# Joining the attention sums with the normalised rows: one addition moves from TensorE to GpSimd

## The chip, the cores and the metric

The kernel runs on one core of one Trainium2 chip. The metric is the device time of one execution in microseconds (us), told as the median of several executions. A core has five engines that run side by side and meet only at semaphores: TensorE (matrix products, into PSUM), VectorE, ScalarE, GpSimd (elementwise work and indirect transfers) and SyncE, which issues transfers here. Profiles call them PE (PEld for its weight loads), DVE, ACT, POOL and SP.

## The reference, cut to what matters

The program is one graph attention layer with a feed-forward network, and then a layer of experts, over 6250 nodes of 256 features. The change touches the place where attention ends and the first batch norm begins:

```python
z      = layernorm(x)                                  # the normalised row of each node
alpha  = ex / (seg_sum[dst] + 1e-16)
out    = segment_sum(alpha * xl[src], dst)             # over the edges, the node's own edge among them
x_attn = out.reshape(n, H * C) + bias
h      = batchnorm(x_attn + z, gamma1, beta1)          # statistics over all nodes
```

So for each node three rows of 256 numbers are added, and the bias: the scaled sum over its edges (`mean` in the kernel), the message of its own edge (`own`), and its normalised row (`z`). What follows wants features on the partitions, so the sum is also turned round: 128 nodes on partitions become 128 nodes along the free dimension.

## The kernel before, in words

The function `join_heads` (line 1208) does this after the attention stage and before `feed_forward`. There are NT = 49 tiles of 128 nodes, taken in pairs of an even and an odd tile: STEPS = 25 steps, the last one with an even tile only. All loops over steps are unrolled. A step i runs over these engines:

- SyncE, `load` (lines 1245 to 1249): two transfers into a ring of four buffers, `xl` (264 KB) and `z` (256 KB). The load of step i waits until step i-4 has been turned.
- VectorE: `scale` (line 1283) multiplies the accumulated sums of both tiles with a factor per head into `mean` (line 1287, one instruction on 128x512). It waits until step i-2 has been turned, since `mean` has two buffers. `odd_messages` (line 1291) makes `own` of the odd tile in four instructions (one per head, line 1298), each of which multiplies and adds `z`: so the odd tile's `z` is already in its `own`. `measure` (line 1301) then takes the batch statistics of step i-2 in two instructions on 128x256 (line 1305).
- ScalarE: `even_messages` (line 1328) makes `own` of the even tile, four scaled copies that can't add `z` (line 1334); `keep` (line 1337) copies the turned result out of PSUM with the bias, two instructions (line 1341). Its order is even messages of step i+1, keep of step i.
- TensorE: `turn` (line 1354) adds and turns at once. Each part is multiplied with the identity, and the products accumulate in PSUM (line 1368). The even tile has three parts (`z`, `mean`, `own`) and the odd tile two (`mean`, `own`), each in two halves of 128 features: ten products a step, (3 + 2) x 2. The profile records each of these float32 products as two instructions.
- GpSimd has nothing to do in this stage.

After the last step VectorE aggregates the statistics and the feed-forward stage begins. An earlier stage, `project_nodes` (lines 480 to 652), matters for the rows further down: there GpSimd adds two float32 tiles of 128x264 in each of 50 rounds (line 535), while VectorE works on the same tiles at lines 547, 553, 557, 565 and 470.

Of the kernel before, what the change touches and what calls it, by code (L numbers as in the profile page):

```python
# [12 lines left out]
ALU = mybir.AluOpType  # L13
# [85 lines left out]
def give_root(nc, k, act, root, var):  # L99

    k.given += 1
    act.wait_ge(k.var_ready, k.given)
    nc.scalar.activation(root, var, ACT.Sqrt).then_inc(k.root_ready, 1)
# [17 lines left out]
def wait_past(engine, semaphore, value):  # L121

    if isinstance(value, int) and value <= 0:
        return
    engine.wait_ge(semaphore, value)
# [1082 lines left out]
def join_heads(nc, k):  # L1208
# [4 lines left out]
    STEPS = (NT + B - 1) // B  # L1213
    RING = 4
    with ExitStack() as ctx:
        sb = lambda name, shape, dt=F32: ctx.enter_context(nc.sbuf_tensor(name, shape, dt))
        pb = lambda name, shape: ctx.enter_context(nc.psum_tensor(name, shape, F32))
        sem = lambda name: ctx.enter_context(nc.semaphore(name))
# [7 lines left out]
        z = sb("j_z", [P, RING, B, D])  # L1226
        own = sb("j_own", [P, 2, B, D])
        mean = sb("j_mean", [P, 2, B, D])
# [6 lines left out]
        z_in = [sem(f"j_z_in{s}") for s in range(RING)]  # L1235
        even_ready, odd_ready, scaled, turned, kept, did = (sem("j_even_s"), sem("j_odd_s"), sem("j_scaled"), sem("j_turned"),
                                                            sem("j_kept"), sem("j_did"))
        heads = lambda a: a.rearrange("p u (h c) -> p u h c", c=C)
        tiles_in = lambda i: min(B, NT - i * B)

        with nc.Block(no_gpsimd_drain=True) as block:

            @block.sync
            def _(sp):
                def load(i, s):
                    wait_past(sp, turned, i - (RING - 1))
                    at = bass.ds(i * (B * P), B * P)
                    sp.dma_start(xl[:, s], k.xl_rows[at, :].rearrange("(u p) w -> p u w", p=P)).then_inc(xl_in[s], 16)
                    sp.dma_start(z[:, s], k.z_rows[at, :].rearrange("(u p) d -> p u d", p=P)).then_inc(z_in[s], 16)

                for i in range(RING):
                    load(i, i)
                with nc.allow_non_contiguous_dma(reason="one number of each feature"):
                    for i, v in enumerate((k.gamma1, k.beta1)):
                        sp.dma_start(par[:, i], v.rearrange("(h p) -> p h", p=P)).then_inc(par_in, 16)
                    sp.dma_start(bias[:, :], k.bias.rearrange("(h p) -> p h", p=P)).then_inc(par_in, 16)

                for w, v in ((k.f_w1, k.W1), (k.f_w2, k.W2)):
                    sp.dma_start(w[:, :, :], v.rearrange("(h p) n -> p h n", p=P)).then_inc(k.ffn_in, 16)
                with nc.allow_non_contiguous_dma(reason="one number of each feature"):  # L1260
                    for out, v in ((k.f_b1[:, :], k.b1), (k.f_b2[:, :], k.b2), (k.f_par[:, 0], k.gamma2), (k.f_par[:, 1], k.beta2)):
                        sp.dma_start(out, v.rearrange("(h p) -> p h", p=P)).then_inc(k.ffn_in, 16)
                for i in range(RING, STEPS):
                    load(i, i % RING)
# [58 lines left out]
            def _(act):  # L1323
# [25 lines left out]
                    keep(i)  # L1349
                give_root(nc, k, act, tmp[:, :, 3], tmp[:, :, 2])  # L1350

            @block.tensor
            def _(pe):
                def turn(i):
                    s, b = i % RING, i % 2
                    pe.wait_ge(z_in[s], i // RING * 16 + 16)
                    pe.wait_ge(scaled, i + 1)
                    wait_past(pe, kept, DH * (i - 1))
                    for u in range(tiles_in(i)):
                        if u == 0:  # L1360
                            pe.wait_ge(even_ready, H * (i + 1))
                            parts = (z[:, s, 0], mean[:, b, 0], own[:, b, 0])
                        else:
                            pe.wait_ge(odd_ready, H * (i + 1))
                            parts = (mean[:, b, 1], own[:, b, 1])
                        for h in range(DH):
                            for n, part in enumerate(parts):
                                last = nc.tensor.matmul(turn_ps[:, b, h, u * P:(u + 1) * P], part[:, h * P:(h + 1) * P], k.ident[:, :],
                                                        start=(n == 0), stop=(n + 1 == len(parts)))
                    last.then_inc(turned, 1)  # L1370

                for i in range(STEPS):
                    turn(i)
# [795 lines left out]
def graph_ffn_kernel(nc, *args):  # L2169
# [21 lines left out]
    with ExitStack() as ctx:  # L2191
# [59 lines left out]
        with ExitStack() as layer:  # L2251
            sb = lambda name, shape, dt=F32: layer.enter_context(nc.sbuf_tensor(name, shape, dt))
            k.f_w1, k.f_w2 = sb("f_w1", [P, DH, D]), sb("f_w2", [P, DH, D])
            k.f_b1, k.f_b2, k.f_par = sb("f_b1", [P, DH]), sb("f_b2", [P, DH]), sb("f_par", [P, 2, DH])
            join_heads(nc, k)
            feed_forward(nc, k)
# [18 lines left out]
```

## Time and profile before

| what | value |
|---|---|
| time, median of 3 runs | 2482.79 us (2479.42 to 2486.21) |
| profiled execution, its own time | 2486.9 us |
| span of the profile | 2485.1 us, 43501 instructions |
| busy: PE, PEld, DVE, ACT, POOL | 78%, 67%, 61%, 48%, 49% of the span |
| the stage of the change | from about 1680 to 1749.6 us after the span's start |

The profile is of one execution; its own time lies 1.8 us around its span (launch and end), and it is 4.1 us over the median of the three runs. The busy shares are means over stages with different limits, so they say little about this stage of 70 us, 2.8% of the span. Of the page's chain of waits only the last transfers of the program are told, so the stage has to be read from its own stretch of the time line.

### The profile page before, as it was taken

To read this page: it belongs to the slowest core of one execution; us is meant where nothing else is said; L and a number is where in the kernel's file an instruction comes from. 1 tells how busy PE (TensorE), PEld (TensorE's weight loads), DVE (VectorE), ACT (ScalarE), POOL (GpSimd) and SP (SyncE) were. 2 spreads that over 40 slices of the span, in tenths; PEclk is the share of its full clock that TensorE was granted. 3 is DMA by queue.
4 is the path that set the end of the run, shared out by engine and by line. 5 is a ranking of instruction groups with operands and counts; after the bars stand their busy time and mean duration, and the time that the engine had idled before them with its cause. 6 is when DMAs were issued, how large, how long until landed. Compare 5 with 4: busy or idle time off the path is not lost. (4 is left out here: it accounts for less than half of the span.)

```text
span 2485.1 us, 43501 instructions
## 1 busy us (share of the span) xinstructions
PE 1949.5 (78%) x9692; PEld 1661.9 (67%) x9693; DVE 1512.5 (61%) x3638; ACT 1193.7 (48%) x2805; POOL 1211.4 (49%) x1207
## 2 busy tenths in 40 slices
PE   2975788788788878877887878888886526999996
PEld 2764667666666766666766666667865526888885
DVE  5964777777777877777777877788456430111110
ACT  2542555555555555555555555566545412323231
POOL 3346656656666555656566656610003561344444
PEclk9987999999999999899999999998985557999998
DMA  7676666666666666666666666627502335666664
GB/s 212 228 251 183 194 191 194 188 189 194 189 190 191 186 186 182 195 187 194 187 197 190 192 183 196 187 61 208 187 7 96 106 126 164 143 140 145 140 146 73
DMA packets 256712, 422.34 MB, mean 170 GB/s; under 512 B 45801, under 2 KB 128088, under 8 KB 256652
## 3 DMA queue, kind: packets, MB, share of 16 engines
q1 hardware_dynamic: 154608, 223.36, 28.7%
q0 software_dynamic: 65408, 153.31, 24.3%
q10 hardware_dynamic: 36636, 45.00, 5.9%
q8 instruction: 23, 0.38, 0.1%
q14 instruction: 37, 0.30, 0.0%
HBM read 358.65 MB, written 62.86 MB: 170 GB/s over the span
## 5 line engine op out<-in xcount | busy, mean ns | idle before, releaser
L824 POOL DMA_INDIRECT ring<-xl_rows,a_idx x928 | 888.1, 957 | 578.8 <-issue 248.5
L1141 PE MATMUL a_f_ps<-a_xr_w,a_hot_n 128*128 128x256 f32 x1856 | 572.5, 391 | 156.4 <-DVE a_pos L999 97.4
L1143 PE MATMUL a_f_ps<-ring,ident 128*128 128x256 f32 x1856 | 588.8, 400 | 3.3 <-issue 3.2
L1156 PE MATMUL a_o_ps<-ring,a_hot_e 128*128 128x264 f32 x1856 | 521.9, 406 | 60.1 <-DVE acc L1036 35.9
L1141 PEld LDWEIGHTS a_f_ps<-a_xr_w,a_hot_n 128*128 128x128 f32 x1856 | 369.2, 203 | 246.3 <-DVE a_pos L999 92.9
L1156 PEld LDWEIGHTS a_o_ps<-ring,a_hot_e 128*128 128x128 f32 x1856 | 364.1, 201 | 140.1 <-issue 79.7
L999 DVE SCALAR_TENSOR_TENSOR a_pos<-a_f_ps,att_cols 128x512 f32<-128x512 f32 x464 | 316.4, 682 | 224.1 <-PE a_f_ps L1143 109.5
L905 ACT ACTIVATE a_hot_e<-a_far_e,one 128x512 f32<-128x512 f32 x232 | 167.6, 722 | 383.6 <-PE a_o_ps L1156 201.0
L1009 DVE TENSOR_REDUCE a_lg<-a_pos 128x8 f32<-128x512 f32 x464 | 316.0, 681 | 34.1 <-remote 33.3
L1023 DVE TENSOR_TENSOR ring<-ring,a_sm_ps (+1 forms) x464 | 315.3, 679 | 1.6 <-issue 1.6
L1143 PEld LDWEIGHTS a_f_ps<-ring,ident 128*128 128x128 f32 x1856 | 303.8, 201 | 3.3 <-issue 3.3
L898 ACT ACTIVATE a_far_e<-iota_row,a_near_rel 128x128 f32<-128x128 f32 x928 | 294.8, 388 | 3.4 <-issue 2.0
L2035 POOL DMA_INDIRECT out_dram<-ring,x_idx x106 | 165.9, 1565 | 262.0 <-issue 125.9
L888 ACT ACTIVATE a_hot_n<-a_far_n,one 128x512 fp32r<-128x512 f32 x232 | 167.5, 722 | 177.7 <-PE a_f_ps L1143 70.9
L1036 DVE TENSOR_TENSOR acc<-a_o_ps,acc 128x264 f32 x464 | 197.5, 426 | 89.5 <-PE a_o_ps L1156 49.7
L2154 DVE CAST x_idx<-ring 128x2 int32<-128x2 f32 x53 | 9.3, 175 | 385.3 <-PE x_y_ps L2081 385.3
L2081 PE MATMUL x_y_ps<-we,ring 128*128 x848 | 191.6, 379 | 0.0
L2071 PE MATMUL x_hid_ps<-ring,x_w 128*128 128x256 f32 x784 | 177.2, 379 | 0.0
L882 ACT ACTIVATE a_far_n<-a_rel_bc,neg_col 128x512 f32<-128x512 bf16 x232 | 164.8, 710 | 25.6 <-issue 22.3
L2081 PEld LDWEIGHTS x_y_ps<-we,ring 128*128 128x128 f32 x848 | 157.1, 190 | 19.3
L2071 PEld LDWEIGHTS x_hid_ps<-ring,x_w 128*128 128x128 f32 x784 | 149.0, 190 | 20.3
L2113 ACT COPY ring<-x_zt_ps 128x512 f32<-128x512 f32 x53 | 31.0, 585 | 248.2 <-PE x_zt_ps L2049 167.4
(349 smaller groups left out, 2169.9 us busy)
## 6 DMA issues: line engine op xcount, KB each, us to landing
a_xr_w<-xr_rows SPq DMA_DIRECT2D x464, 256.0 KB
a_rel_bc<-rel_rows ACTq DMA_DIRECT2D x116, 256.0 KB
x_w<-in_L_ffn_W_dram SPq DMA_DIRECT2D x57, 512.0 KB, 4.4
ring<-xl_rows,a_idx POOLq DMA_INDIRECT x928
xr_rows<-xr_parts SPq DMA_DIRECT2D x50, 256.0 KB, 2.1
ring<-disp_rows SPq DMA_DIRECT2D x49, 257.0 KB
xl_rows<-xl_sb SPq DMA_DIRECT2D x50, 132.0 KB, 1.8
j_xl<-xl_rows SPq DMA_DIRECT2D x25, 264.0 KB, 3.0
```

The lines of the kernel that those rows point to most:

```text
L824: nc.gpsimd.indirect_dma_start(xl_e[:, p * T + 2 * h + u, :], None, k.xl_rows, bass.IndirectOffsetOnAxis(ap=idx[:, p, 2 * h + u:2 * h + u ...
L898: nc.scalar.activation(far_e[:, u, :], k.iota_row[:, :], ACT.Abs, bias=near_rel[:, j * QT + u:j * QT + u + 1]).then_inc(far_e_ready, 1)
L905: nc.scalar.activation(hot_e[:, j % 2], far_e[:, :, :], ACT.Relu, scale=-1.0, bias=k.one[:, 0:1]).then_inc(hot_e_ready, 1)
L999: nc.vector.scalar_tensor_tensor(pos[:, h % 2], f_ps[:, slot(h)], 0.0, att, ALU.max, ALU.mult).then_inc(settled, 1)
L1009: nc.vector.tensor_reduce(lg[:, :, 2 * h:2 * h + 2].rearrange("p h t -> p t h"), pos[:, h % 2].rearrange("p t (h c) -> p t h c", c=C), AX. ...
L1023: nc.vector.tensor_tensor(at[:, :, :, 0:C], at[:, :, :, 0:C], exs_of(sm)[:, 2 * hh:2 * hh + 2, :, None].to_broadcast([P, 2, H, C]), ALU.mu ...
L1036: nc.vector.tensor_tensor(at, o_ps[:, slot(hh), 0:XW], at, ALU.add).then_inc(added, 1)
L1141: nc.tensor.matmul(f_ps[:, slot(h), u, :], hot_n[:, j % 2, 2 * g + u, :], xr_w[:, h % XR, a, :].bitcast(F32R), start=(a == 0), stop=False)
L1143: last = nc.tensor.matmul(in_heads(f_ps[:, slot(h), u, :]), k.ident[:, :], heads_of(xl_e[:, p * T + 2 * h + u, :])[:, :, 0:C], start=False ...
L1156: last = nc.tensor.matmul(o_ps[:, slot(hh), 0:XW], hot_e[:, j % 2, 2 * g + u, :], xl_e[:, pp * T + 2 * hh + u, :], start=(u == 0), stop=(u ...
L2071: last = nc.tensor.matmul(hid_ps[:, q % 2, j], w1[:, q % RING, h, j * P:(j + 1) * P], zt[:, q % 2, h], start=(h == 0), stop=(h == DH - 1))
L2081: last = nc.tensor.matmul(y_ps[:, q % 2, u], hid[:, q % 2, j, u * P:(u + 1) * P], k.we2[:, bass.ds(e[u], 1), j, :].rearrange("p o n -> p ( ...
```

## The change

GpSimd gets a block in this stage. In each step it waits for the scaled sums and for the rows `z`, adds the even tile's `z` to the even tile's `mean` in place, and signals a new semaphore. TensorE waits for that semaphore in place of `scaled` and of the transfer of `z`, and multiplies two parts of the even tile with the identity in place of three. The odd tile, VectorE's, ScalarE's and SyncE's programs are as before.

```diff
+        joined = sem("j_joined")
...
+            @block.gpsimd
+            def _(pool):
+                def join(i):
+                    s, b = i % RING, i % 2
+                    pool.wait_ge(scaled, i + 1)
+                    pool.wait_ge(z_in[s], i // RING * 16 + 16)
+                    nc.gpsimd.tensor_tensor(mean[:, b, 0], mean[:, b, 0], z[:, s, 0], ALU.add).then_inc(joined, 1)
+
+                for i in range(STEPS):
+                    join(i)
+
             @block.tensor
             def _(pe):
                 def turn(i):
-                    s, b = i % RING, i % 2
-                    pe.wait_ge(z_in[s], i // RING * 16 + 16)
-                    pe.wait_ge(scaled, i + 1)
+                    b = i % 2
+                    pe.wait_ge(joined, i + 1)
                     wait_past(pe, kept, DH * (i - 1))
                     for u in range(tiles_in(i)):
                         if u == 0:
                             pe.wait_ge(even_ready, H * (i + 1))
-                            parts = (z[:, s, 0], mean[:, b, 0], own[:, b, 0])
+                            parts = (mean[:, b, 0], own[:, b, 0])
```

## Rows read from the trace of the kernel before

**Rows 1.** Windows over the stage. Columns: stretch, length, busy (count) of each engine.
```profile
core 0: us, PE busy (x) PEld busy (x) DVE busy (x) ACT busy (x) POOL busy (x), PEclk, DMA share, GB/s
1691.00:1695.70 4.70, 4.35 (x22) 4.38 (x23) 0.00 (x1) 1.16 (x6) 0.00 (x0) 0.55 0.00 0
1700.00:1720.00 20.00, 20.00 (x182) 20.00 (x181) 19.16 (x64) 16.05 (x54) 0.00 (x0) 1.00 0.82 238
```
**Rows 2.** Time line of VectorE in one step. Columns: start, us, engine, line, operation, count, [idle before].
```profile
1700.16 0.69 DVE L1287 TENSOR_TENSOR j_mean<-acc,j_over 128x512 f32<-128x512 f32 x1
1700.77 0.87 DVE L1298 SCALAR_TENSOR_TENSOR j_own<-j_xl,j_share,j_z 128x64 f32<-128x64 f32 x4
1701.56 0.75 DVE L1305 BATCH_NORM_STATS2 j_stats<-ring 128x6 f32<-128x256 f32 x2
1702.40 0.69 DVE L1287 TENSOR_TENSOR j_mean<-acc,j_over 128x512 f32<-128x512 f32 x1
```
**Rows 3.** Time line of ScalarE in the same step.
```profile
1700.16 0.84 ACT L1341 ACTIVATE ring<-j_turn_ps,j_bias 128x256 f32<-128x256 f32 x2 [0.45 <-PE j_turn_ps L1368]
1700.89 1.06 ACT L1334 ACTIVATE j_own<-j_xl,j_share 128x64 f32<-128x64 f32 x4
```
**Rows 4.** Time line of TensorE: first instructions of two turns that follow one another.
```profile
1699.96 0.39 PE L1368 MATMUL j_turn_ps<-ident,j_z 128*128 128x128 f32 x2
...
1702.20 0.39 PE L1368 MATMUL j_turn_ps<-ident,j_z 128*128 128x128 f32 x2
```
**Rows 5.** The tile j_z: its instructions (ns min/median/max), and its transfers.
```profile
L1368 PE MATMUL j_turn_ps<-ident,j_z x100: 275/275/552, 1691.3 to 1747.6; 128*128 128x128 f32 x100
L1298 DVE SCALAR_TENSOR_TENSOR j_own<-j_xl,j_share,j_z x96: 278/281/281, 1686.6 to 1743.8; 128x64 f32<-128x64 f32 x96
DMA to landing us min/median/max: 3.0/3.2/5.8
```
**Rows 6.** The beginning of the stage: time line of all engines.
```profile
1687.35 0.69 DVE L1287 TENSOR_TENSOR j_mean<-acc,j_over 128x512 f32<-128x512 f32 x1
1687.95 0.87 DVE L1298 SCALAR_TENSOR_TENSOR j_own<-j_xl,j_share,j_z 128x64 f32<-128x64 f32 x4
1690.14 2.02 ACT L1334 ACTIVATE j_own<-j_xl,j_share 128x64 f32<-128x64 f32 x8 [7.25 <-DMA j_bias<-in_L_gnn_bias_dram]
1691.35 0.77 PE L1368 MATMUL j_turn_ps<-ident,j_z 128*128 128x128 f32 x2 [12.32 <-ACT j_own L1334]
1695.70 0.69 DVE L1287 TENSOR_TENSOR j_mean<-acc,j_over 128x512 f32<-128x512 f32 x1 [6.88 <-PE j_turn_ps L1368]
```
**Rows 7.** The end of the stage: time lines of VectorE and of ScalarE.
```profile
1744.83 0.43 DVE L1287 TENSOR_TENSOR j_mean<-acc,j_over 128x256 f32<-128x256 f32 x1
1745.70 0.75 DVE L1305 BATCH_NORM_STATS2 j_stats<-ring 128x6 f32<-128x256 f32 x2 [0.45 <-ACT ring L1341]
1747.94 0.75 DVE L1305 BATCH_NORM_STATS2 j_stats<-ring 128x6 f32<-128x256 f32 x2 [1.48 <-ACT ring L1341]
1749.06 0.44 DVE L1305 BATCH_NORM_STATS2 j_stats<-ring 128x6 f32<-128x106 f32 x2 [0.37 <-ACT ring L1341]
1748.40 0.62 ACT L1341 ACTIVATE ring<-j_turn_ps,j_bias 128x128 f32<-128x128 f32 x2 [0.50 <-PE j_turn_ps L1368]
```
**Rows 8.** Lines of the projection stage: durations of GpSimd's addition and VectorE's instructions beside it.
```profile
L535 POOL TENSOR_TENSOR f_sb<-xl_sb,xr_sb x50: 739/838/1007, 57.0 to 165.0; 128x264 f32<-128x264 f32 x50
L547 DVE TENSOR_SCALAR z_sb<-ring,ln_mean,ln_rstd x50: 407/834/941, 50.7 to 159.2; 128x256 f32<-128x256 f32 x26, 128x256 f32 x24
L470 DVE BATCH_NORM_STATS2 ln_stats<-ring x50: 405/416/428, 16.5 to 104.0; 128x6 f32<-128x256 f32 x50
```
**Rows 9.** Time line of the projection stage, a round in which GpSimd comes before line 547.
```profile
63.26 0.41 DVE L565 TENSOR_TENSOR xr_parts<-xr_sb,xr_parts 128x256 fp32r<-128x256 f32 x1
63.36 0.92 POOL L535 TENSOR_TENSOR f_sb<-xl_sb,xr_sb 128x264 f32<-128x264 f32 x1 [1.18 <-ACT xr_sb L604]
63.59 0.84 DVE L547 TENSOR_SCALAR z_sb<-ring,ln_mean,ln_rstd 128x256 f32<-128x256 f32 x1
```
**Rows 10.** The same stage, a round in which line 547 comes before GpSimd.
```profile
130.05 0.42 DVE L565 TENSOR_TENSOR xr_parts<-xr_sb,xr_parts 128x256 fp32r<-128x256 f32 x1
130.38 0.41 DVE L547 TENSOR_SCALAR z_sb<-ring,ln_mean,ln_rstd 128x256 f32 x1
130.52 0.87 POOL L535 TENSOR_TENSOR f_sb<-xl_sb,xr_sb 128x264 f32<-128x264 f32 x1 [1.46 <-ACT xr_sb L604]
```
**Rows 11.** Windows in the attention stage, for the granted clock beside TensorE's busy time.
```profile
1410.00:1420.00 10.00, 6.70 (x38) 5.41 (x37) 8.94 (x26) 6.13 (x14) 5.72 (x6) 1.00 0.67 211
1640.00:1660.00 20.00, 14.61 (x60) 11.65 (x59) 16.27 (x42) 10.00 (x27) 0.00 (x0) 0.86 0.00 0
```

## The prediction

> **What bounds the stage now.** I read the windows over the stage first. Between 1700 and 1720 us TensorE is busy all 20 us at the full granted clock (1.00, its level of 2.4 GHz), VectorE 19.16, ScalarE 16.05, GpSimd nothing [rows 1]. So TensorE is the bound, with VectorE close behind. The time lines then give the step. Two turns that follow one another start at 1699.96 and 1702.20 [rows 4], and two `scale` instructions at 1700.16 and 1702.40 [rows 2]; over 22 steps, from 1695.70 [rows 6] to 1744.83 [rows 7], the step is 49.13 / 22 = 2.233 us. TensorE spends it on ten products, 20 recorded instructions: 0.1117 us each (each lasts 0.275 [rows 5], but they are pipelined).
>
> How close VectorE is: with no wait it needs, start to start, 0.61 for `scale`, 0.79 for the four odd messages (1701.56 - 1700.77), and for the two statistics twice the 0.34 by which the second starts behind the first (0.75 for two, less one duration of 0.41 [rows 2, 8]). That is 2.07 us. It has 0.16 us to spare in a step. ScalarE waits 0.45 us in each step for TensorE [rows 3]. A cheaper turn alone can therefore win only about 0.16 us a step, then VectorE is the bound: this is the reading on which all below rests.
>
> **The change, part by part.**
>
> *TensorE.* One part of the even tile goes: two products in each of 25 steps, the 100 recorded instructions on `j_z` [rows 5]. A turn is then 16 instructions, 16 x 0.1117 = 1.79 us, 0.45 less. That takes TensorE off the path in the steady part.
>
> *GpSimd.* It adds 25 additions of 128x256. The nearest row is its addition of 128x264: 0.74 us at the least, 0.84 median [rows 8]; I take 0.72 without obstruction (0.74 x 256/264) and up to 0.97 where it has to wait for VectorE. GpSimd has no other work here, so its own time costs nothing if the loop through it is short enough. The loop is: `scale` 0.69, about 0.07 for the semaphore, addition 0.97, 0.07, turn 1.79, 0.07 = 3.66 us, and `mean` has two buffers, so it allows a step of 1.83 us. Not the bound. (The 0.07 is the gap from the end of a copy on ScalarE to line 535 in the projection stage.) What is queued behind TensorE's new wait are only its own turns. A step's loads go out when the turn four steps back ends, two steps (4.5 us) ahead of their use, and land in 3.2 us [rows 5]; a longer step gives them more room.
>
> *VectorE beside GpSimd.* No instruction of VectorE's changes, but the addition always starts when `scale` ends, that is during the odd messages, and these read two tiles (`xl` and `z`). The projection stage shows what the two engines do to one another. In [rows 9] line 565 ends at 63.67; GpSimd, which had started at 63.36, ends at 64.28, 0.61 later and 0.92 long; line 547, queued directly behind line 565, takes 0.84 instead of 0.41 and ends at 64.43, 0.76 after line 565. In [rows 10], where line 547 starts ahead of GpSimd, it ends (130.79) 0.32 after line 565 (130.47), with 0.41. So GpSimd steps in between two VectorE instructions, and the second is held back by 0.76 - 0.32 = 0.44 us. The medians of all rounds agree: 0.834 against a least of 0.407 is 0.43 [rows 8]. In the new order the addition is over (about 1.7 us after `scale` starts) before the statistics begin (1.4 + 0.43 = 1.8), so only the odd messages meet it.
>
> The trace has no instruction with two tiles of input that was held back by GpSimd, only one (line 565) behind which GpSimd waited, which says that they use something in common. So the cost to the odd messages is bounded from both sides: 0 a step (they are not held, or GpSimd waits until the statistics), and 0.72 (held for the addition's whole time). A gain below nothing is excluded, since VectorE does the same instructions. I take 0.43, from the row of the one case of holding that is measured.
>
> The Trainium skill says it as a rule ("SBUF — State Buffer", Who interferes with whom): GpSimd and VectorE share one pair of ports, a VectorE instruction with two SBUF inputs contends with a GpSimd instruction that reads SBUF, and the later one is blocked for the whole instruction of the other. The first half agrees with lines 535 and 565; the second would give 0.72 us a step where the rows give 0.43. It is a rival below.
>
> *The sum.* The new step is VectorE's: 2.07 + 0.43 = 2.50 us, 0.27 more than now. Over 22 steps: +5.9 us.
>
> The start: the first turn begins at 1691.35, when ScalarE's even messages of step 0 are there (they waited for the bias's transfer until 1690.14), and `scale` of step 2 gets away at 1695.70 [rows 6]. TensorE had stood idle for 12 us, and the granted clock is 0.55 on average there [rows 1]: 1.2 GHz nearly to the end. The first two additions are long done by 1691 (VectorE has finished step 1 at 1688.8 [rows 6], plus 0.43 and an addition). The first turn becomes 16 instructions at 0.213 (the 0.1117 at half the clock, less rounding) and 0.1 for the signal, 3.5 us instead of 4.35: -0.85 us.
>
> The end: from the last `scale` (1744.83) to the end of the last statistics (1749.50) it is 4.67 us [rows 7], since TensorE still owes a turn and a half. Afterwards TensorE is ahead: 0.43 for `scale` of one tile, 0.07, 0.72 addition, 0.07, eight instructions 0.89, 0.1, `keep` 0.62, 0.05, statistics 0.44 = 3.4 us: -1.3 us.
>
> Together 5.9 - 0.85 - 1.3 = +3.75, or +3.8 us. The profiled execution would go from 2486.9 to 2490.7; set against the median of the three runs, which is 4.1 us lower, 2482.8 + 3.8 = 2486.6 us. By the lower bound (no holding) it is 22 x (2.07 - 2.233) = -3.6, with the ends -5.7 us; by the upper one 22 x (2.79 - 2.233) = +12.3, with the ends +10.1 us. By the skill's rule the sum would be that upper one.
>
> A change of this kernel can be told from none from about 0.3% on, 7.4 us. The forecast of +3.8 us (+0.15%) is within it.
>
> **The rivals.**
>
> *Slower: VectorE stands for the whole addition in every step.* Place: the first odd messages behind each `scale`; price 0.72 us a step, +10.1 us, 2492.9 us (0.86 by the mean of line 535 would make it +13). It decides from 0.60 us of holding on: 22 x (2.07 + 0.60 - 2.233) - 2.15 = +7.5. For it: the longest line 547 is 0.941, 0.53 over its least, and the odd messages are a kind that the trace doesn't show held. Against it: in the round of [rows 9] GpSimd is active for 0.61 us after line 565, and VectorE loses only 0.44, since its own start-up overlaps the wait.
>
> *GpSimd gives way, and runs under the statistics.* The odd messages come so close on one another that GpSimd might get in only behind the fourth. It would then run from about 1.4 to 2.0 us after `scale`'s start, under the statistics, and if these, with one tile of input, aren't held (no row shows them beside an addition), VectorE would keep its 2.07 us. The turn would end at 2.0 + 0.07 + 1.79 = 3.9 us, just inside the two steps of 4.14 that the buffers allow. -5.7 us, 2477.1 us. Against it: in [rows 9] an instruction already queued directly behind another lost to GpSimd.
>
> *TensorE's clock falls.* Now it is busy without a break; then 1.79 of 2.50 us, 72%. Stretches of the attention stage with 67% keep a full clock, others with 73% in which it stood for longer show 0.86 [rows 11]. At 1.2 GHz a turn takes 16 x 0.213 = 3.4 us and the step with it; if that held for the whole stage, 22 x (3.4 - 2.233) = +26 us, 2509 us; for half of it some +15. Against it: the breaks are of 0.7 us only.
>
> **How the numbers follow.** The forecast 0.60; VectorE held for the whole addition 0.22; GpSimd under the statistics 0.13; the clock 0.05. The range goes from the lower bound, 2477, to somewhat beyond the upper one, 2497, which leaves out the clock and the tails. Slower by over 0.3%: the first rival almost wholly (0.20), the clock (0.05) and a little of the forecast (0.03), 0.28. Faster by over 0.3% needs more than the lower bound gives, and the help of the measurement: 0.05. Within 0.3%: 0.67.
>
> **What would show each step.** TensorE's idle time: about 0.7 us before each turn, released by VectorE's or GpSimd's work, and 16 instructions a step. `scale` to `scale` at 2.50 us, with no wait ahead of it on VectorE; 2.07 would mean no holding, 2.8 the whole. One of the four odd messages at about 0.7 us instead of 0.28, the statistics still at 0.41. Line 1358's addition at 0.72 to 0.97 us. The first turn at 3.5 us. The stage's end at about 1753.3 instead of 1749.6. A step set by TensorE again (its idle time gone, clock below 1), or GpSimd's addition far above 1 us, would make the reading wrong.

## The result and the profile after

The changed kernel takes 2485.64 us in the median of 22 runs (2481.85 to 2491.89), the kernel before on the same chip 2482.05 (2475.54 to 2488.10). The ratio is 1.0017, with a 95% interval of 1.0010 to 1.0024: +4.2 us (2.5 to 6.0), slower, but by less than the 0.3% named ahead (the two medians alone are 3.6 us apart). The forecast was +3.8 us. The profiled execution of the changed kernel took 2491.89 us, with a span of 2490.1 us, 5.0 more than before.

The windows over the stage have turned round against [rows 1]. Columns as there.

```profile
core 0: us, PE busy (x) PEld busy (x) DVE busy (x) ACT busy (x) POOL busy (x), PEclk, DMA share, GB/s
1691.00:1695.70 4.70, 4.70 (x24) 4.70 (x25) 0.95 (x3) 1.72 (x7) 0.18 (x1) 0.55 0.00 0
1700.00:1720.00 20.00, 16.17 (x128) 14.65 (x128) 20.00 (x56) 14.37 (x50) 5.78 (x8) 1.00 0.73 215
```

VectorE is busy without a break, 20.00 us where it was 19.16, and completes fewer instructions, 56 for 64. TensorE now has breaks (16.17 for 20.00), still at a granted clock of 1.00, and GpSimd is there with eight additions. The time line of one step, all engines, against [rows 2 to 4]:

```profile
1715.02 0.67 DVE L1288 TENSOR_TENSOR j_mean<-acc,j_over 128x512 f32<-128x512 f32 x1
...
1715.62 1.35 DVE L1299 SCALAR_TENSOR_TENSOR j_own<-j_xl,j_share,j_z 128x64 f32<-128x64 f32 x4
...
1715.77 0.72 POOL L1359 TENSOR_TENSOR j_mean<-j_mean,j_z 128x256 f32<-128x256 f32 x1 [1.81 <-DVE j_mean L1288]
...
1716.55 0.49 PE L1379 MATMUL j_turn_ps<-ident,j_mean 128*128 128x128 f32 x2 [0.48 <-POOL j_mean L1359]
...
1716.89 0.74 DVE L1306 BATCH_NORM_STATS2 j_stats<-ring 128x6 f32<-128x256 f32 x2
...
1717.55 0.67 DVE L1288 TENSOR_TENSOR j_mean<-acc,j_over 128x512 f32<-128x512 f32 x1
```

From `scale` to `scale` it is 2.53 us, with no wait of VectorE in between. The addition begins 0.15 us after the odd messages' first, and four messages last 1.35 us instead of 0.87; all else on VectorE has its old length within 0.02 us. Which of the messages pays is seen in the instructions by tile (ns, min/median/max), against [rows 5]:

```profile
L1299 DVE SCALAR_TENSOR_TENSOR j_own<-j_xl,j_share,j_z x96: 269/273/774, 1686.2 to 1749.6; 128x64 f32<-128x64 f32 x96
```

The median is 273 where it was 281, and the longest is 774: the whole is on one of the four. In each of the 24 steps with odd messages it is the second, the first to start after the addition. The same step with that message by itself:

```profile
1715.77 0.72 POOL L1359 TENSOR_TENSOR j_mean<-j_mean,j_z 128x256 f32<-128x256 f32 x1 [1.81 <-DVE j_mean L1288]
1715.81 0.77 DVE L1299 SCALAR_TENSOR_TENSOR j_own<-j_xl,j_share,j_z 128x64 f32<-128x64 f32 x1
```

The addition ends at 1716.49 and the message at 1716.58, some 0.08 us behind it; a message that is not held lasts 0.27 us from its own start. The beginning and the end of the stage, against [rows 6, 7]:

```profile
1690.96 0.77 PE L1379 MATMUL j_turn_ps<-ident,j_mean 128*128 128x128 f32 x2 [12.34 <-ACT j_own L1335]
...
1694.75 0.69 DVE L1288 TENSOR_TENSOR j_mean<-acc,j_over 128x512 f32<-128x512 f32 x1 [5.35 <-PE j_turn_ps L1379]
...
1750.43 0.40 DVE L1288 TENSOR_TENSOR j_mean<-acc,j_over 128x256 f32<-128x256 f32 x1
...
1753.55 0.44 DVE L1306 BATCH_NORM_STATS2 j_stats<-ring 128x6 f32<-128x106 f32 x2 [0.41 <-ACT ring L1342]
1754.09 1.70 DVE L1199 BATCH_NORM_AGGREGATE j_tmp<-j_stats 128x2 f32<-128x150 f32 x2
```

Call the stage the time from the first `scale` to the first aggregation of the statistics. It was 63.66 us and is 68.53, +4.87, which is the 5.0 us of the span within 0.2. In three parts: first to third `scale` 9.75 to 9.19 (-0.56), 22 steps of 2.233 to 22 of 2.531 (+6.55), last `scale` to aggregation 4.78 to 3.66 (-1.12).

### The profile page after: what moved, and what is told of

It reads as the page before. It is cut to its first block and busy times, and to the rows that moved or that the text cites. A ratio compares the mean times of both kernels' runs of the same rounds, so it can differ in the third digit from the quotient of the medians.

```text
span 2490.1 us, 43328 instructions
## 1 busy us (share of the span) xinstructions
PE 1946.6 (78%) x9592; PEld 1656.5 (67%) x9593; DVE 1522.5 (61%) x3638; ACT 1194.8 (48%) x2805; POOL 1229.6 (49%) x1232
```

## The experiments

Ratios are against the kernel before on the same chip in the same session; that kernel's own median lay between 2454 and 2491 us from session to session, so times of different sessions aren't compared. The stage (as above) is read from each profile. Its beginning depends on when the bias lands: TensorE first starts between 4.4 and 6.0 us after the first `scale`, so up to 1.6 us between two stages can come from that alone. The column "from TensorE" leaves it out: it counts from TensorE's first product to the same end.

| kernel | step, us | stage, us | from TensorE, us | ratio (95% interval) |
|---|---|---|---|---|
| before | 2.233 | 63.66 | 58.26 | 1 |
| changed | 2.531 | 68.53 | 63.12 | 1.0017 (1.0010 to 1.0024) |
| no addition | 2.04, two longer | 58.45 | 52.46 | 0.9971 (0.9961 to 0.9981) |
| second input from PSUM | 2.02, three longer | 57.72 | 53.24 | 0.9973 (0.9961 to 0.9985) |
| side addition 128x256 | 2.513 | 67.64 | 62.91 | 1.0008 (0.9997 to 1.0019) |
| side addition 128x512 | 3.055 | 79.76 | 75.02 | profile only |
| side memset 128x512 | 2.233 | 62.96 | 58.53 | profile only |
| addition after the odd messages | 2.239 | 62.64 | 57.36 | 0.9986 (0.9973 to 0.9999) |
| the same again | 2.239 | 62.90 | 57.35 | 0.9992 (0.9982 to 1.0002) |
| and three buffers | 2.19 | 61.65 | 55.79 | 0.9996 (0.9986 to 1.0006) |
| three buffers alone | 2.53 | 67.64 | 62.13 | profile only |
| half the addition | 2.04 to 2.96 | 62.00 | 56.61 | 0.9996 (0.9987 to 1.0006) |
| and five buffers for loads | 2.04 and 2.17 | 59.37 | 54.53 | 0.9979 (0.9969 to 0.9989) |

**No addition.**

```diff
-                            parts = (z[:, s, 0], mean[:, b, 0], own[:, b, 0])
+                            parts = (mean[:, b, 0], own[:, b, 0])
```

> The kernel before with the even tile's z left out of the sum altogether: TensorE multiplies two parts, and there is no addition on GpSimd (the output lacks this term). It shows the step without the two engines' meeting. My theory (VectorE is the next bound, and only the addition holds it up): step 2.05 to 2.07 us against 2.233, start -0.55, end -1.2, in all -5.6 us against the kernel before, ratio 0.9977, and no odd message longer than 0.28 us. Rival (the changed kernel's step of 2.53 us comes from a longer loop through semaphores and buffers, or from ScalarE, and not from a held VectorE): the step stays near 2.23 us or more and VectorE shows idle time.

Time line of VectorE in one step:

```profile
1711.33 0.67 DVE L1287 TENSOR_TENSOR j_mean<-acc,j_over 128x512 f32<-128x512 f32 x1
1711.92 0.87 DVE L1298 SCALAR_TENSOR_TENSOR j_own<-j_xl,j_share,j_z 128x64 f32<-128x64 f32 x4
1712.70 0.75 DVE L1305 BATCH_NORM_STATS2 j_stats<-ring 128x6 f32<-128x256 f32 x2
1713.37 0.41 DVE L1287 TENSOR_TENSOR j_mean<-acc,j_over 128x256 f32<-128x256 f32 x1
```

2.04 us: VectorE's floor, and the gain that TensorE's smaller turn is worth by itself, 0.2 us a step, 0.29% in all. So the saving is real, and the addition costs all of it and more. Two of the steps here were longer, 2.39 and 2.44; in the second VectorE stood for a transfer of `z`. That comes back below.

**Second input from PSUM.** The odd messages add a zeroed PSUM tile in place of `z`.

```diff
-                                                       z[:, s, 1, at], ALU.mult, ALU.add).then_inc(odd_ready, 1)
+                                                       zero_ps[:, at], ALU.mult, ALU.add).then_inc(odd_ready, 1)
```

> The changed kernel with the odd messages' second input taken from a zeroed tile in PSUM in place of z in SBUF (so the odd tile's z is left out). Their number, form and place beside the addition stay. Theory (the second input from SBUF is what they share with GpSimd): four of them take 0.87 to 0.95 us again, step 2.05 to 2.15 us, -5 us against before, ratio 0.998. Rival (the addition slows or holds any VectorE instruction that is queued behind another): 1.35 us for four as in the changed kernel, step 2.53 us, ratio 1.0017.

Time line of VectorE and GpSimd:

```profile
1710.35 0.84 DVE L1301 SCALAR_TENSOR_TENSOR j_own<-j_xl,j_share,j_zero_ps 128x64 f32<-128x64 f32 x4
1710.50 0.73 POOL L1361 TENSOR_TENSOR j_mean<-j_mean,j_z 128x256 f32<-128x256 f32 x1 [1.29 <-DVE j_mean L1290]
```

The addition starts 0.15 us after the first message, as in the changed kernel, and the four take 0.84. So the messages meet the addition only when both of their inputs lie in SBUF. That is not a rule for all of VectorE's instructions: line 547 of the projection stage has one tile of input and is held [rows 9].

**A side addition**, which nobody waits for, beside the kernel before: 128x256, then 128x512, then an instruction that only writes.

```diff
+            @block.gpsimd
+            def _(pool):
+                nc.gpsimd.memset(side[:, :, :], 0.0).then_inc(side_ready, 1)
+                for i in range(STEPS):
+                    pool.wait_ge(side_ready, i + 1)
+                    pool.wait_ge(scaled, i + 1)
+                    nc.gpsimd.tensor_tensor(side[:, 0, 0:256], side[:, 1, 0:256], side[:, 2, 0:256], ALU.add).then_inc(side_ready, 1)
```

> The kernel before, with its three parts on TensorE, and beside it an addition of 128x256 on GpSimd of tiles that nobody else uses, released by each scale instruction. It pays the cost without the gain. Theory (VectorE sets the step once it is held, TensorE's saving is hidden): step 2.53 us, as in the changed kernel, though a turn still takes 2.23; in all 22 x 0.30 = +6.6, less up to 0.7 at the end, +6 us against before, ratio 1.0024; the odd messages at 1.35 us for four. Rival (the cost of the change is its longer chain scale, addition, turn): nobody waits for this addition, so the step stays at 2.23 us and the ratio at 1.000.

> The kernel before with an addition of 128x512 on tiles that nobody else uses, in place of 128x256 as in the run with the side addition (there 0.84 us on GpSimd, 0.46 us of holding). Theory (VectorE is held for the addition's length less a fixed start-up of 0.25 to 0.4 us): the addition takes 1.3 to 1.45 us, the odd messages 0.87 + 1.05 = 1.9 us for four, the step 3.1 us. Rival (a hold has a fixed price, about 0.48 us for each meeting): 1.35 us for four, step 2.53 us.

> The kernel before with a GpSimd instruction that only writes: a memset of 128x512 in its own tile, released by each scale. Theory (what is shared is the reading side): odd messages at 0.87 us for four, step 2.23 us, time as before (ratio 1.000), although GpSimd is active at the same moment. Rival (any GpSimd instruction on SBUF holds VectorE): odd messages longer by the memset's length less some 0.25 us, step 2.3 to 2.6 us.

Time lines of VectorE and GpSimd, with the held message by itself (x1), 128x256:

```profile
1713.14 1.33 DVE L1300 SCALAR_TENSOR_TENSOR j_own<-j_xl,j_share,j_z 128x64 f32<-128x64 f32 x4
...
1713.36 0.84 POOL L1360 TENSOR_TENSOR j_side<-j_side 128x256 f32<-128x256 f32 x1 [1.67 <-DVE j_mean L1289]
...
1713.53 0.75 DVE L1300 SCALAR_TENSOR_TENSOR j_own<-j_xl,j_share,j_z 128x64 f32<-128x64 f32 x1
...
1725.65 0.73 POOL L1360 TENSOR_TENSOR j_side<-j_side 128x256 f32<-128x256 f32 x1 [1.41 <-DVE j_mean L1289]
```

128x512:

```profile
1691.51 1.88 DVE L1300 SCALAR_TENSOR_TENSOR j_own<-j_xl,j_share,j_z 128x64 f32<-128x64 f32 x4
...
1691.73 1.38 POOL L1360 TENSOR_TENSOR j_side<-j_side 128x512 f32<-128x512 f32 x1 [1.68 <-DVE j_mean L1289]
...
1691.90 1.30 DVE L1300 SCALAR_TENSOR_TENSOR j_own<-j_xl,j_share,j_z 128x64 f32<-128x64 f32 x1
```

the memset:

```profile
1692.25 0.87 DVE L1300 SCALAR_TENSOR_TENSOR j_own<-j_xl,j_share,j_z 128x64 f32<-128x64 f32 x4
...
1692.45 0.52 POOL L1360 MEMSET j_side<- 128x512 f32 x1 [1.71 <-DVE j_mean L1289]
```

An addition that is in nobody's chain gives the changed kernel's step, 2.51 us, with TensorE's three parts still in place: in the changed kernel TensorE's saving is wholly hidden behind a VectorE that is held. An addition longer by 0.54 us (1.38 for 0.84) holds it longer by 0.55 (1.88 for 1.33): the price is the addition's length less a part that doesn't grow with it, 0.38 here and 0.24 in the changed kernel.

The instructions one by one say what that part is. In the changed kernel and with both side additions, in each of the 24 steps with odd messages, one message is held, the first that starts after the addition, and it ends 0.08 to 0.09 us after the addition's end. So VectorE loses the time from where this message would have ended to where it does. In the changed kernel the addition starts 0.16 us after the first message, so it holds the second, which would have ended at 0.47 and ends at 0.96. In the side runs it starts at 0.22, just after the second has started, so it holds the third, which would have ended at 0.67 and ends at 1.14 (1.69 with 128x512). Here the addition itself also takes longer: the last one, with no messages beside it, is 0.73 us long and not 0.84 (1.27 and not 1.38 with 128x512).

The memset holds nobody. With the PSUM input this says that what the two share lies in reading SBUF; a GpSimd instruction that computes without reading SBUF was not run. One number missed: the whole, +2.0 us by the ratio (+4.0 by the stage) for +6 expected. The stage's end became 1.46 us shorter (I had allowed 0.7), and its beginning was 0.7 us shorter, the bias having landed sooner after the first `scale`.

**Addition after the odd messages.**

```diff
                     pool.wait_ge(scaled, i + 1)
+                    pool.wait_ge(odd_ready, H * min(i + 1, NT // 2))
```

> The changed kernel with one more wait on GpSimd: it adds only when the four odd messages are done, so under the batch statistics, which read one tile. Theory (only instructions with two inputs from SBUF are held): odd messages back at 0.87 us for four, statistics at 0.41 each although the addition runs beside them, step 2.08 to 2.15 us (the loop 0.69 + 0.71 + 0.1 + 0.72 + 0.07 + 1.79 + 0.07 = 4.15 us for two steps allows 2.08), in all about -3.8 us against before, ratio 0.9985. Rival (GpSimd holds whatever VectorE does): the 0.48 us move from the odd messages to the statistics, the step stays at 2.5 us and the time at +4 us, ratio 1.0017.

> The addition after the odd messages with two buffers once more, on the same chip as the half addition, since its interval (0.9973 to 0.9999) was wide for a stage that was only 1.0 us shorter than before. By the stage alone the ratio should be 0.9996 (step 2.24 us, alternately 2.19 and 2.29); if it is 0.9985 again, something outside the stage differs.

Time line, all engines, from one `scale` to the one two steps on:

```profile
1709.89 0.70 DVE L1288 TENSOR_TENSOR j_mean<-acc,j_over 128x512 f32<-128x512 f32 x1
...
1710.51 0.86 DVE L1299 SCALAR_TENSOR_TENSOR j_own<-j_xl,j_share,j_z 128x64 f32<-128x64 f32 x4
...
1711.29 0.74 DVE L1306 BATCH_NORM_STATS2 j_stats<-ring 128x6 f32<-128x256 f32 x2
...
1711.50 0.72 POOL L1360 TENSOR_TENSOR j_mean<-j_mean,j_z 128x256 f32<-128x256 f32 x1 [1.46 <-DVE j_own L1299]
...
1712.28 0.49 PE L1380 MATMUL j_turn_ps<-ident,j_mean 128*128 128x128 f32 x2
...
1714.37 0.69 DVE L1288 TENSOR_TENSOR j_mean<-acc,j_over 128x512 f32<-128x512 f32 x1
```

Neither the messages (0.86) nor the statistics (0.74 for two) are held, though the addition runs beside the latter: the expectation holds for these two. But the step is 2.24 us, not 2.1: the loop through two buffers now binds. It takes 4.48 us (1.61 to the addition's start, 0.72, 0.06, a turn of 2.02 with its last product's latency, 0.07 for the signal). I had put it at 4.15. The second timing, 0.9992, suits the stage better than the first: from TensorE's first product it is 0.9 us shorter than before.

**Three buffers for `mean` and `own`**, with that order and without it.

```diff
-        own = sb("j_own", [P, 2, B, D])
-        mean = sb("j_mean", [P, 2, B, D])
+        own = sb("j_own", [P, 3, B, D])
+        mean = sb("j_mean", [P, 3, B, D])
...
-                    wait_past(dve, turned, i - 1)
+                    wait_past(dve, turned, i - 2)
```

> The addition after the odd messages, as in the run before it, and mean and own with three buffers in place of two, so that scale and the messages wait for the turn three steps back. In the run with two buffers the loop scale 0.70, odd messages to 1.61, addition 0.72, 0.06, turn 2.02, 0.07 took 4.48 us for two steps. Theory (held VectorE and that loop are the only two things that cost the change its gain): step 2.05 to 2.10 us, stage 58 to 59 us against 63.7 before, -5 us, ratio 0.998 or somewhat lower; it would beat both kernels. Rival (something else is next, the transfers of z first of all, for which VectorE stood 0.3 us once in the run without an addition): step 2.2 us or more, ratio 0.9985 to 1.000.

> The changed kernel with three buffers for mean and own, but the addition where the change has it, beside the odd messages. Theory (VectorE, held 0.48 us a step, is the bound, not the loop): step 2.53 us as in the changed kernel, four odd messages at 1.35 us, no gain from the buffers. Rival (the loop through scale, addition and turn sets the changed kernel's step): 2.1 to 2.3 us.

Without the order the step is 2.53 us: the buffers were not what bound the changed kernel. With it, the time line of VectorE and GpSimd:

```profile
1692.66 0.73 POOL L1360 TENSOR_TENSOR j_mean<-j_mean,j_z 128x256 f32<-128x256 f32 x1 [1.47 <-DVE j_own L1299]
1693.11 0.83 DVE L1288 TENSOR_TENSOR j_mean<-acc,j_over 128x512 f32<-128x512 f32 x1
```

This missed: 2.19 us, ratio 0.9996. The loop is gone, but the addition, 0.73 us long from 0.22 us after the statistics began, reaches past their 0.67 us into the next `scale`, which has two inputs from SBUF and takes 0.83 in place of 0.67: it ends 0.55 us after the addition in each of 20 steps.

**Half the addition**, so that it fits: GpSimd takes one half of the features, TensorE the other as a third part; then a fifth buffer for the loads.

```diff
-                    nc.gpsimd.tensor_tensor(mean[:, b, 0], mean[:, b, 0], z[:, s, 0], ALU.add).then_inc(joined, 1)
+                    nc.gpsimd.tensor_tensor(mean[:, b, 0, 0:P], mean[:, b, 0, 0:P], z[:, s, 0, 0:P], ALU.add).then_inc(joined, 1)
...
+                            if u == 0 and h == 1:
+                                parts = (z[:, i % RING, 0],) + parts
```

> Three buffers and the addition after the odd messages, but GpSimd adds only the first 128 of the even tile's 256 features; TensorE takes z as a third part for the other 128 (nine products a turn in place of eight or ten). In the run with the whole addition it took 0.73 us from 0.22 us after the statistics began, reached past their 0.67 us, and scale took 0.83 us instead of 0.67. Theory (only what lies beside a two-input instruction costs): an addition of about 0.45 us ends inside the statistics, scale is back at 0.67 us, TensorE needs 9 x 0.2235 = 2.01 us, VectorE's 2.05 us is the step; stage 58 to 60 us, -4 to -5 us, ratio 0.998. Rival (transfers of z or TensorE's nine products with their semaphores are next): step 2.15 us or more and a ratio above 0.999.

> The half addition (three buffers, after the odd messages) with five buffers in place of four for the loads of xl and z, so that a load waits for the turn five steps back. In the half addition 11 of 21 steps took 2.03 to 2.04 us, and ten were longer, up to 2.96, with transfers of z landing late. Theory (the step of 2.04 is VectorE's, the rest were late transfers of z, for want of a buffer): nearly all steps 2.04 us, stage 58.5 to 59.5 us in place of 62.0, -4.5 us against before, ratio 0.998. Rival (the transfers can't keep up at all at 520 KB in 2.04 us, whatever they wait for): as many long steps as before, stage 61 us or more, ratio 0.9996.

With four buffers for the loads the time didn't move: `scale` is back at 0.67 us and twelve steps take 2.04, but nine are longer, up to 2.96 (my count ahead of the next run was one off), among them four in which VectorE stood for a transfer of `z` (1.7 us in all; the longest wait is below). With five (`RING = 5`, the first four loads issued ahead of the parameters as before) the steps are alternately 2.04 and 2.17 us, and no wait for `z` is left on VectorE. In the steps of 2.17 the statistics start 0.13 us later, 0.03 us after ScalarE's copy of the turned result has ended: they wait for it. The wait with four buffers; then, with five, the time line and a window:

```profile
1704.65 0.87 DVE L1299 SCALAR_TENSOR_TENSOR j_own<-j_xl,j_share,j_z 128x64 f32<-128x64 f32 x4 [0.83 <-DMA j_z<-z_rows]
```

```profile
1716.52 0.68 DVE L1288 TENSOR_TENSOR j_mean<-acc,j_over 128x512 f32<-128x512 f32 x1
...
1718.11 0.46 POOL L1360 TENSOR_TENSOR j_mean<-j_mean,j_z 128x128 f32<-128x128 f32 x1 [1.71 <-DVE j_own L1299]
1718.55 0.68 DVE L1288 TENSOR_TENSOR j_mean<-acc,j_over 128x512 f32<-128x512 f32 x1
```

```profile
1710.00:1730.00 20.00, 20.00 (x173) 19.42 (x172) 19.77 (x67) 16.77 (x58) 4.24 (x10) 1.00 0.86 251
```

The ratio is 0.9979 (0.9969 to 0.9989), 5.2 us (2.7 to 7.7) under the kernel before: this version beats both (the changed kernel by way of the kernel before: the two were not timed in one session). TensorE and VectorE are both full, 20.00 and 19.77 of 20 us.

## Why the prediction was right

- *TensorE bounds, VectorE next with 2.07 us.* Right. Without an addition the step is 2.04.
- *VectorE is held by the addition, 0.43 us a step.* The mechanism was right in its place (one of four messages, nothing else), and its size was 0.48, 0.05 short. The row behind it was of line 547, a kind with one tile of input, so that the sizes came so near was in part luck: what is alike is that both end a fixed time after the addition, line 547 0.15 us (41 of its 50 rounds), a message 0.08. How long the loss is depends on where the addition happens to start. That the messages need their second input from SBUF for it was open in the trace of before; the PSUM input (0.84 us for four) shows it.
- *The step: 2.50 us.* It was 2.531, so 22 steps gave +6.55 for +5.9. VectorE's own need was put 0.03 too high and the holding 0.05 too low. TensorE's wait before a turn is 0.48 us, for about 0.7 forecast.
- *The first turn: -0.85 us.* It was -0.56. The changed turn was summed up as 16 x 0.213 + 0.1 and compared with a measured 4.35; the measured one holds some 0.4 us of start and latency of its last product, of which I gave the new one 0.1. 1690.96 to 1694.75 is 3.79 us, not 3.5. Seen from the other side: the two products that go would have cost 0.85 us at the lower clock, but the old turn ran its last two faster (0.55 and 0.39 us the pair in the trace in place of 0.63), and the new one was over before.
- *The end: -1.3 us.* It was -1.12.
- *Sum.* +3.75 forecast, +4.87 in the profiled pair, +4.2 (2.5 to 6.0) by the ratio. The three parts were all short, by 0.65, 0.29 and 0.18 us. The ratio's interval can't tell the two sums apart; the profile does.
- *The rival "held for the whole addition", 0.72 us a step*: its price is false, 0.48 of 0.72 us and 1.01 of 1.38. But the held message does stand until the addition is over: it ends 0.08 to 0.09 us behind it, in all 72 steps of three kernels. The loss is shorter than the addition because the message starts after it and would have needed some of that time in any case. The Trainium skill ("SBUF — State Buffer", Who interferes with whom) says that two inputs from SBUF contend with a GpSimd instruction that reads SBUF, and that whoever comes second is blocked for the whole instruction of the first. The trace agrees with both for the messages; what did not follow from it was a loss of the addition's whole length.
- *The rival "GpSimd gives way"*: false in the changed kernel, where it got in between two messages in each step. Made to happen by a wait, it gave 2.24 us and not the 2.07 I had priced, and the loop bound: the addition ended 2.33 us after `scale`'s start for the 2.0 I had put, and the turn takes 2.02 with its latency for 1.79.
- *The clock*: 1.00 between 1700 and 1740 us with TensorE at 81%. It did not fall.

What stays open: why the addition starts 0.16 us after the first message in the changed kernel and 0.22 in the side runs, which decides the message that is held; and why line 547 is held with one tile of input and the batch statistics, with one too, are not.

## What to carry to other kernels

Work taken off the bounding engine is worth the distance to the next engine, here 0.2 of 0.45 us a step; look at who is next before deciding who receives the work. GpSimd's idle time is not free where VectorE is that next engine: beside a GpSimd addition on SBUF, a VectorE instruction of the kinds that are held ends only after the addition has ended, and here that took all of the addition's length but 0.24 to 0.38 us. Held were the messages and `scale`, both with two inputs from SBUF, and line 547 with one; not held were the statistics and the messages with their second input from PSUM. So the number of inputs alone doesn't settle it: look in the trace for the kind beside a GpSimd instruction. Put the addition beside kinds that are not held, see that it ends before the next one that is, and count the buffers of the longer loop, the loads' among them.

## What the runs showed that I had not expected

- The version that gained 5.2 us has four changes on top: the order, a third buffer, half the addition and a fifth buffer for the loads. They were added one after the other; that it needs all four was not tested by taking one out. Of the first two, the order alone gave 0.9986 and 0.9992 (its second interval includes 1), and the order with the third buffer 0.9996: each removed a bound and met the next within 0.05 to 0.2 us.
- GpSimd comes between two VectorE instructions that are queued back to back, between the first message and the second, in every one of the changed kernel's 24 steps with odd messages. The steps are as even: 2.52 to 2.56 us over the 22 from the third `scale` on.
- A step of 2.04 us wants 520 KB of loads in that time. The version without an addition drew 268 GB/s between 1690 and 1710 us at a DMA share of 0.92, and four buffers for loads, enough at 2.23 us, let some steps wait. The window (columns as in [rows 1]):

```profile
1690.00:1710.00 20.00, 19.48 (x161) 18.30 (x159) 20.00 (x69) 17.84 (x60) 0.00 (x0) 1.00 0.92 268
```

- That the engines meet only at semaphores is too simple: the side addition shares no tile with VectorE and signals no semaphore that it waits for, and costs it 0.46 us a step.
